# Three threshold points instead of two for each tile of a nucleus search, with two and three VectorE evaluations instead of three and four

## The reference

```python
Q = Xa @ W1;  K = Xa @ W3
logits = Q @ W2 @ K.T
idx = jnp.argsort(-logits, axis=1)
csum = jnp.cumsum(softmax(take_along_axis(logits, idx)), axis=1)
k_i = jnp.sum(csum < P_NUC, axis=1) + 1          # P_NUC = 0.9
A = softmax(where(rank < k_i, logits, -inf))     # the kept ones only
Xf = Rf @ Xf;  Xb = Rb @ Xb;  Xa = A @ Xa        # two steps
Z = Z + (Xf @ U1[s] + Xb @ U2[s] + Xa @ U3[s])
```

## Time and profile before

| what | us |
| --- | --- |
| median of three runs | 3486.06 (3485.86 to 3487.74) |
| profiled execution, time | 3488.64 |
| profiled execution, span | 3486.8 |
| TensorE busy | 3144.3 (90%) |
| VectorE busy | 2454.0 (70%) |
| GpSimd busy | 2146.4 (62%) |
| ScalarE busy | 1599.1 (46%) |

### The profile page before, as it was taken

One profiled execution on the slowest core, in us unless ns is written; L12 is line 12 of the kernel. 1 busy time (PEld: TensorE's weight loads), 2 busy tenths in 40 slices (PEclk: granted clock), 3 DMA queues, 4 the chain that ended last, 5 costly groups with the idle time before them and its releaser, 6 DMA issues. The chain is left out here.

```text
span 3486.8 us, 42119 instructions
## 1 busy us (share of the span) xinstructions
PE 3144.3 (90%) x13212; PEld 2272.6 (65%) x13212; DVE 2454.0 (70%) x3451; ACT 1599.1 (46%) x2357; POOL 2146.4 (62%) x4214
## 2 busy tenths in 40 slices
PE   4999989998699999999976698988899999996899
PEld 3788878885477777777754254544566566664788
DVE  6983410002998889888884799999978999998000
ACT  2211321225566666666653455555555655552200
POOL 1212421124788888888880677877988788886211
PEclk9999999998899999999988899999999999998899
DMA  6643444443122122112211111211222222223254
GB/s 246 223 162 132 130 147 163 163 142 86 44 58 58 58 58 66 54 59 63 65 33 62 47 52 52 62 44 56 57 81 76 73 84 82 74 83 102 91 201 172
DMA packets 140702, 327.59 MB, mean 94 GB/s; under 512 B 15456, under 2 KB 93664, under 8 KB 129248
## 3 DMA queue, kind: packets, MB, share of 16 engines
q1 hardware_dynamic: 140512, 325.30, 29.3%
HBM read 286.70 MB, written 38.54 MB: 93 GB/s over the span
## 5 line engine op out<-in xcount | busy, mean ns | idle before, releaser
L1027 ACT ACTIVATE junk<-E,negp 128x3327 uint8<-128x3327 f32 x208 | 637.3, 3064 | 142.4 <-issue 107.8
L1399 DVE SCALAR_TENSOR_TENSOR U<-E,trial 128x3327 f32<-128x3327 f32 x182 | 678.5, 3728 | 0.0
L922 PE MATMUL bank<-big,adj 128*128 128x512 f32 x1352 | 609.9, 602 | 8.7 <-ACT t L1053 8.7
L922 PEld LDWEIGHTS bank<-big,adj 128*128 128x128 f32 x1352 | 252.9, 192 | 329.2 <-issue 328.1
L294 PE MATMUL bank<-big,E 128*128 128x256 f32 x1664 | 366.2, 381 | 2.4 <-PEq L58 1.7
L882 PE MATMUL bank<-Hc,PT 128*128 128x256 f32 x1248 | 305.1, 396 | 69.2 <-ACT PT L1066 69.2
L294 PEld LDWEIGHTS bank<-big,E 128*128 128x128 f32 x1664 | 315.9, 191 | 49.3 <-issue 6.6
L882 PE MATMUL bank<-Hc,adj 128*128 128x256 f32 x1456 | 335.4, 382 | 10.7 <-ACT adj L1066 10.7
L1361 DVE TENSOR_REDUCE nmax<-E 128x1 f32<-128x3327 f32 x52 | 188.0, 3615 | 207.4 <-ACT E L1070 207.4
L882 PEld LDWEIGHTS bank<-Hc,PT 128*128 128x128 f32 x1248 | 245.9, 199 | 129.9 <-ACT PT L1066 79.7
L882 PEld LDWEIGHTS bank<-Hc,adj 128*128 128x128 f32 x1456 | 277.8, 191 | 72.9 <-issue 23.0
(11 more groups left out here) (248 smaller groups left out, 5937.2 us busy)
## 6 DMA issues: line engine op xcount, KB each, us to landing
adj<-adjT SPq DMA_DIRECT2D x131, 448.0 KB, 3.4
E<-adjT SPq DMA_DIRECT2D x32, 1664.0 KB, 6.9
adj<-adjT SPq DMA_DIRECT2D x104, 384.0 KB, 3.4
adj<-adjT SPq DMA_DIRECT2D x20, 1664.0 KB, 7.0
E<-adjT SPq DMA_DIRECT2D x26, 1216.0 KB, 5.7
xt<-xin SPq DMA_DIRECT2D x52, 128.0 KB, 5.7
x_d<-xn SPq DMA_DIRECT2D x52, 128.0 KB, 1.7
xt<-x_d SPq DMA_DIRECT2D x52, 128.0 KB, 5.2
```

Source lines behind the costliest of these rows:

```text
L922: last = mm(agg[:, 0:w], adj[:, SPAN * (k % 2) + j - AGG[k]], rhs[:, j], start=(j == 0), stop=False)
L1027: go(junk[:, 0:N], E[:, t % DEPTH, 0:N], func, bias=negp[:, t % 2, j:j + 1], scale=1.0, accum_out=acc_[:, t % 2, j:j + 1]).then_inc(summed ...
L1399: V_.scalar_tensor_tensor(out=U[:, 0:N], in0=e, scalar=point, in1=e, op0=ALU.is_ge, op1=ALU.mult, accum_out=found))
```

## The change

`POINTS` goes from 2 to 3 in both steps, and `EVALS` from (3, 4) to (2, 3). ScalarE gets a fifth pass per tile: point 2 has a count pass only, in slot 2 ahead of point 0 of the next tile, and point 1's Relu pass moves from slot 0 to slot 1. One semaphore `summed` counts all passes. GpSimd gets `update(R, 2)` just before `update(F, 0)`, and `update` is rewritten: it corrects the negated point at once in five (point 0) or eight (points 1 and 2) dependent steps after the last sum, and does the bracket afterwards; for point 1 it also prepares a two-sided estimate, since point 2 has no Relu pass. Some constants differ. The core of the diff:

```diff
-EVALS = (3, 4)
+EVALS = (2, 3)
-POINTS = 2
+POINTS = (3, 3)
...
         def sums(t, j, m):
-            if m == 0:
-                act.wait_ge(aimed[j], t + 1)
-                if j > 0:
-                    act.wait_ge(summed[j - 1], PASSES[j - 1] * (t + 1))
...
+            if m == 0 or j == 2:
+                act.wait_ge(aimed[j], tiles_with(t, j))
+            if nth[t, j, m] > 1:
+                act.wait_ge(summed, nth[t, j, m] - 1)
...
-                if k == 0 and R is not None:
-                    sums(R, 1, 0)
...
                     if R is not None:
+                        sums(R, 1, 0)
                         sums(R, 1, 1)
...
+                    if R is not None and POINTS[R // NT] > 2:
+                        sums(R, 2, 1)
                     if F is not None:
                         sums(F, 0, 0)
...
         def prepare(t):
-            then(ts(up[:, q, 0:2], known[:, 4 + 2 * step:6 + 2 * step], p, ga[:, q, 12:13], ALU.mult, ALU.add),
-                 ts(up[:, q, 3:4], p, p, RIDGE[step] ** 2, ALU.mult, ALU.mult))
-            then(tt(up[:, q, 4:5], up[:, q, 3:4], ga[:, q, 11:12], ALU.mult))
+            then(ts(up_(2), p, N / 2 + AIM[step], ga[:, q, 12:13], ALU.mult, ALU.add),
+                 ts(up[:, q, 0:2], known[:, 4 + 2 * step:6 + 2 * step], p, None, ALU.mult),
+                 ts(up_(3), p, p, RIDGE[step] ** 2, ALU.mult, ALU.mult))
+            then(tt(up_(4), up_(3), ga[:, q, 11:12], ALU.mult))
...
+            then(ts(cand[:, q, 0:1], p, 1.0, None, ALU.mult))
             prepare(t)
...
         def update(t, j):
-            pool.wait_ge(summed[j], PASSES[j] * (t + 1))
-            then(ts(count, sign[:, q, j:j + 1], 0.5, N / 2, ALU.mult, ALU.add))
-            then(ts(mass_, count, p, over[:, q, j:j + 1], ALU.mult, ALU.add))
...
+            if j < 2:
+                pool.wait_ge(summed, nth[t, j, 0])
+                then(tt(up_(5), over[:, q, j:j + 1], up_(2), ALU.add))
+            pool.wait_ge(summed, nth[t, j, 1])
+            if j < 2:
+                then(ts(slip, signs, up_(0), up_(5), ALU.mult, ALU.add))
+            else:
+                then(ts(slip, signs, up_(16), up_(17), ALU.mult, ALU.add))
+            if j == 0:
+                then(ts(up_(13), slip, slope, STRIDE, ALU.mult, ALU.min))
+            else:
+                then(tt(up_(7), slip, up_(6), ALU.subtract))
+                then(ts(up_(8), up_(7), up_(7), up_(3), ALU.mult, ALU.add),
+                     ts(up_(9), up_(7), up_(10), up_(4), ALU.mult, ALU.add))
+                then(tt(up_(11), up_(8), minus, ALU.pow),
+                     tt(up_(12), up_(9), slip, ALU.mult))
+                then(ts(up_(13), up_(12), up_(11), STRIDE, ALU.mult, ALU.min))
+            then(ts(up_(14), up_(13), -STRIDE, None, ALU.max))
+            then(tt(up_(15), e_, up_(14), ALU.pow))
+            if not last:
+                then(tt(negp[:, q, j + 1:j + 2], negp[:, q, j:j + 1], up_(15), ALU.mult))
+                pool.sem_inc(aimed[j + 1], 1)
+            if j < 2:
+                then(ts(took[:, 1:2], slip, up_(1), None, ALU.is_ge),
+                     tt(up_(21), up_(15), p, ALU.mult))
+            else:
+                then(ts(up_(18), signs, up_(19), up_(20), ALU.mult, ALU.add),
+                     tt(up_(21), up_(15), p, ALU.mult))
+                then(ts(took[:, 1:2], up_(18), 0.0, None, ALU.is_ge))
+            then(ts(took[:, 0:3:2], took[:, 1:2].to_broadcast([P, 2]), -1.0, 1.0, ALU.mult, ALU.add))
+            then(tt(parts[:, 0], ends, wide(took[:, 0:2]), ALU.mult),
+                 tt(parts[:, 1], cand[:, q].unsqueeze(1).to_broadcast([P, 2, 2]), wide(took[:, 1:3]), ALU.mult))
+            then(tt(ends, parts[:, 0], parts[:, 1], ALU.add))
+            if last:
+                then(ts(point, up_(21), hi, lo, ALU.min, ALU.max))
                 pool.sem_inc(bracketed, 1)
+                return
+            if j == 1:
+                then(tt(up_(22), slip, up_(1), ALU.subtract),
+                     tt(up_(23), signs, up_(0), ALU.mult),
+                     ts(up_(19), p, 0.5, None, ALU.mult),
+                     tt(up_(25), up_(21), p, ALU.add),
+                     tt(up_(26), up_(21), p, ALU.subtract),
+                     tt(slope, up_(9), up_(11), ALU.mult))
+                then(tt(up_(20), up_(22), up_(23), ALU.subtract),
+                     ts(up_(16), up_(25), 0.25, None, ALU.mult),
+                     ts(up_(27), up_(26), AIM[step], slip, ALU.mult, ALU.add))
+                then(tt(up_(28), signs, up_(16), ALU.mult))
+                then(tt(up_(17), up_(27), up_(28), ALU.subtract))
+            then(ts(cand[:, q, 0:1], up_(21), hi, lo, ALU.min, ALU.max),
+                 ts(p, up_(21), 1.0, None, ALU.mult),
+                 ts(up_(6), slip, 1.0, None, ALU.mult),
+                 ts(up_(10), up_(14), -1.0, None, ALU.mult))
+            prepare(t)
...
+            if R is not None and POINTS[R // NT] > 2:
+                update(R, 2)
             if F is not None:
                 update(F, 0)
```

More of the change, by code:

```diff
@@ L18 @@
 TOP = 8
-EVALS = (3, 4)
+EVALS = (2, 3)
 MARKED = -1.0
-PASSES = (2, 2)
-POINTS = 2
[L24 to L27, removed]
+POINTS = (3, 3)
+SHIFT = (1.2, 0.0)
+AIM = (2.0, 4.0)
+KEEP_END = (0.8, 0.85)
 RIDGE = (8.0, 4.0)
@@ L32 @@
 STRIDE = 1.5
-UNDER = 1.0 - 2.0 ** -22
+UNDER = 1.0 - 2.0 ** -20
 SLOTS = 4
@@ L652, in build @@
             over = ab("over", [P, 2, 2])
-            sign = ab("sign", [P, 2, POINTS])
-            negp = ab("negp", [P, 2, POINTS])
+            sign = ab("sign", [P, 2, 3])
+            negp = ab("negp", [P, 2, 3])
             known = ab("known", [P, 8])
             outset = ab("outset", [P, 2, 2, 2])
-            ga = ab("ga", [P, 2, 20])
-            up = ab("up", [P, 2, 24])
-            cand = ab("cand", [P, 2, 3])
+            ga = ab("ga", [P, 2, 16])
+            up = ab("up", [P, 2, 32])
+            cand = ab("cand", [P, 2, 2])
             took = ab("took", [P, 3])
@@ L709, in build @@
             kept = len(spread)
+            passes = []
+            for i in range(rounds):
+                R, F = aim_at(i), exp_at(i)
+                if R is not None:
+                    passes += [(R, 1, 0), (R, 1, 1)] + [(R, 2, 1)] * (POINTS[R // NT] - 2)
+                if F is not None:
+                    passes += [(F, 0, 0), (F, 0, 1)]
+            tiles_with = lambda t, j: sum(POINTS[x // NT] > j for x in range(t + 1))
+            nth = {which: i + 1 for i, which in enumerate(passes)}
             turned = lambda i: sum(first(sent_at(k)) or first(post_at(k)) for k in range(i))
@@ L744, in build @@
                 search, rnd = s("search_step"), s("round_step")
-                summed = [s(f"summed{j}") for j in range(POINTS)]
-                aimed = [s(f"aimed{j}") for j in range(POINTS)]
+                summed = s("summed")
+                aimed = [s(f"aimed{j}") for j in range(3)]
                 step_done, bracketed = s("aim_step"), s("bracketed")
@@ L1170, in _ @@
                         ts = G_.tensor_scalar
-                        KNOWN = (1.0 / ROOT, -1.0, 0.5, float(np.e), AIM[0], STEER[0], AIM[1], STEER[1])
+                        KNOWN = (1.0 / ROOT, -1.0, 0.5, float(np.e), 0.5, AIM[0], 0.5, AIM[1])
                         values = [(known[:, i:i + 1], value) for i, value in enumerate(KNOWN)]
@@ L1191, in restart @@
                             n[0] = 0
-                        def offer(t, j):
-                            then(ts(negp[:, t % 2, j:j + 1], cand[:, t % 2, 0:1], -UNDER, None, ALU.mult))
-                            pool.sem_inc(aimed[j], 1)
                         def prepare(t):
                             q, step = t % 2, t // NT
-                            p = cand[:, q, 0:1]
-                            then(ts(up[:, q, 0:2], known[:, 4 + 2 * step:6 + 2 * step], p, ga[:, q, 12:13], ALU.mult, ALU.add),
-                                 ts(up[:, q, 3:4], p, p, RIDGE[step] ** 2, ALU.mult, ALU.mult))
-                            then(tt(up[:, q, 4:5], up[:, q, 3:4], ga[:, q, 11:12], ALU.mult))
+                            up_ = lambda a: up[:, q, a:a + 1]
+                            p = up_(24)
+                            then(ts(up_(2), p, N / 2 + AIM[step], ga[:, q, 12:13], ALU.mult, ALU.add),
+                                 ts(up[:, q, 0:2], known[:, 4 + 2 * step:6 + 2 * step], p, None, ALU.mult),
+                                 ts(up_(3), p, p, RIDGE[step] ** 2, ALU.mult, ALU.mult))
+                            then(tt(up_(4), up_(3), ga[:, q, 11:12], ALU.mult))
                         def guess(t):
@@ L1209, in guess @@
                             tgt, below = (trial2[:, d, a:a + 1] for a in (GOAL, BELOW))
-                            p = cand[:, q, 0:1]
+                            p = up[:, q, 24:25]
                             pool.wait_ge(exp_done, t + 1)
@@ L1226, in guess @@
                             then(tt(p, e_, ga_(14), ALU.pow))
-                            offer(t, 0)
```

(37 more changed lines are left out.)

6 lines of the change are left out of this document (1 added, 5 removed).

## The result

The changed kernel takes 3871.78 us (median of four runs, 3871.33 to 3874.86) against 3486.09 for the kernel before: a ratio of 1.1107 (95% interval 1.1088 to 1.1126), 385.7 us more. The forecast was 3805, range 3735 to 3940. The profiled execution's span is 3873.1 against 3486.8.

A forecast was written before the change was run, and what follows sets the result against it. GpSimd was taken as full in step 1, side by side with TensorE in step 2's full round; +10.4 work less 3.4 hold gives +7.0 per full round. Terms 161 + 133 + 25 = +319: 3805 us, range 3735 to 3940.

The forecast's parts named there:

- The chain from GpSimd's point over ScalarE's pass to TensorE's copy: Sign in step 1 rounds: TensorE standing some 9 us, mostly for ScalarE's copies; VectorE's idle above 10 us.
- The full round: Step 2 base: full round from 48.8 to 55.8 us; the earlier mean was 49.75, put down to extra removal passes.
- The hold: GpSimd stands about 3.4 us beside each VectorE SCALAR_TENSOR_TENSOR; one evaluation less per tile gives -3.4 us.
- The handover: Point 2's sums take ScalarE about 12 us; GpSimd has 13.6 us of other work, so no wait is added.
- Rival (c): GpSimd also waits for ScalarE at the third handover, 3 us per round: 3940 us; 13% chance.
- Rival (d): Holds on GpSimd shrink to three instead of four or five per round: 3652 us; 6% chance.
- Rival (e): Third point doesn't replace an evaluation, VectorE's removal passes multiply to four per step 2 tile: 3893 us; 3% chance.
- Own work per tile: GpSimd's added work in guess, prepare and the updates, for 39 more instructions: +10.4 us per tile.
- Filling and draining: At start, two changes of step and end, +6 us each: 25 us in total, bounds 0 and 50.
- The upper bound of 13.9 us: GpSimd's added work per tile if all 39 instructions cost the round's mean of 0.356 us; used for the high end.

The follow-up runs named there:

- the ten steps: Kernel before plus ten dependent, useless GpSimd steps at the end of guess, 2.75 us per tile: 3586.6 us, ratio 1.0287.
- the pair of passes with one and two inputs: Changed kernel plus one unused VectorE pass per tile before the pass below the bracket: 4057.95 us with two tile inputs, 3885.78 with one.

## Why the prediction was right

**Which engine.** GpSimd read as full from its timeline, not from its share: shown by the ten steps (+2.7 us per round of step 1 for 2.75 us of work). The chain from GpSimd's point over ScalarE's pass to TensorE's copy grew as forecast: in the round shown TensorE stands 8.43 us where some 9 were given, and VectorE 14.66 where above 10 were given. The full round was also the right base for step 2: the 1 us by which the mean lay above it before is gone (56.85 on the mean, 57.0 in a full round).

**The hold.** 3.4 us per SCALAR_TENSOR_TENSOR, one less per tile: measured 13.0 us for four, 3.25 each, and shown by the pair of passes with one and two inputs. The holds of a round of step 1 so fell by 3.9 us (16.9 to 13.0), not 3.4.

**The handover.** Rival (c) did not come: GpSimd doesn't wait, and the order of ScalarE's passes doesn't matter. ScalarE had point 0's sums 11.2 us after point 2 was offered (12 given), and GpSimd had other work for 14.4 us (1610.40 to 1624.82; 13.6 given). Rival (d) did not come either: every such pass met GpSimd. Rival (e) neither: 72 passes.

**Where the 67 us between 3805 and 3872 lie.** Two terms were sized too low.

- Own work per tile: +10.4 forecast, +11.8 measured. `update(R, 1)` 1606.49 to 1616.85 = 10.4 (10.0 forecast), `update(R, 2)` 1618.67 to 1624.82 = 6.15 (5.9), `update(F, 0)` 1624.82 to 1641.40 less three holds of 10.0 = 6.5 (6.0 before, +0.1 forecast), `guess` 1641.40 to 1653.35 less one hold of 2.9 = 9.0 (8.45 before, +0.3 forecast). With 0.5 us given back by the holds, full rounds became 8.0 and 8.2 us longer, not 7.0: step 1 +184 for 161, step 2 +156 for 133.
- Filling and draining: +47 for 25, close to the upper bound of 50. Between tiles 25 and 29 alone lie +34 for 12, half of them before tile 26, where step 1 drains, and half behind it, where step 2 fills. In the second half GpSimd waited 26.3 us for ScalarE in the kernel before, 17.27 of it ahead of tile 29, and 2.9 in the changed one: the added work used up this waiting and went on past it.

The upper bound of 13.9 us, the mean price of all instructions, was too careful: the added ones are among the cheap.

## What to carry to other kernels

Look at an engine's timeline for gaps that another engine ended, before believing its share: an engine at 62% of the span was full in most rounds of its layer, because over half of such a round was small steps with their turnaround and the rest was holds, which the profile books as work. Before pricing work that is taken away, count the rounds in which the engine waits already. Where one engine holds another, price a moved step by the holds it adds or removes, not by its own length; here a VectorE pass of two inputs cost some 3.5 us on the engine it stopped, and the same length with one input cost nothing. And when a search trades evaluations of one engine for corrections of another, first find out which of the two is full.

## What the runs showed of the hardware

After TensorE's stand of 8.43 us its clock is at the lower of its two levels. TensorE and clock before the stand, right behind it, and later (columns as in the earlier trace rows):

```profile
1606.00:1609.00 3.00, 3.00 (x14) 2.47 (x13) 0.00 (x0) 0.00 (x0) 2.33 (x9) 1.00 0.00 0
1617.80:1622.60 4.80, 4.77 (x12) 3.85 (x13) 3.62 (x1) 4.80 (x7) 3.85 (x11) 0.55 0.01 2
1622.70:1632.00 9.30, 9.30 (x51) 7.39 (x49) 7.04 (x15) 5.66 (x6) 8.13 (x13) 1.00 0.33 95
```

The granted clock goes from 1.00 to a mean of 0.55, close to the lower level of 1.2 GHz out of 2.4, and back to 1.00. The twelve matmuls after the stand take 4.94 us; with the stand of 1.94 in the earlier trace rows twelve took 2.86. The group that holds these matmuls is busy 404.2 us, against 305.1 in the kernel before, for the same 1248 instructions:

```profile
L889 PE MATMUL bank<-Hc,PT 128*128 128x256 f32 x1248 | 404.2, 490 | 374.4 <-ACT PT L1069 374.3
```

These 99 us are about as much as TensorE's 100 us more busy time. That they cost nothing here is argued and not shown by a run of its own: in the rounds TensorE waits for GpSimd's points, and GpSimd for nobody.
